# Opening of a two-layer expert and attention kernel: layer statistics of tiles 2 to 4 set earlier on VectorE, one weight row of the first tile spread by ScalarE, and ScalarE's copy of w2 set behind it

## What is computed

```python
def expert_layer(xt):                       # xt: 8192 x 128, normalised
    scores = sigmoid(xt @ gate_w.T)         # 16 experts
    _, idx = top_k(scores + gate_b, 4)
    w = take_along_axis(scores, idx)
    w = w / sum(w) * 2.5
    comb = zeros(T, 16).at[rows, idx].add(w)
    y = 0
    for e in range(16):
        gate, up = split(xt @ w13[e].T)     # 64 each
        y = y + comb[:, e] * ((silu(gate) * up) @ w2[e].T)
    return y + shared_expert(xt)

x = x + 0.5 * expert_layer(layernorm(x))
x = x + attention(layernorm(x))
x = x + 0.5 * expert_layer(layernorm(x))
```

## Time and profile before

| | |
|---|---|
| median of 3 runs | 842.72 us (842.61 to 843.36) |
| the profiled execution | 843.58 us, of which its span is 841.8 us |
| TensorE busy | 828.7 us (98%) |
| VectorE busy | 723.9 us (86%) |
| ScalarE busy | 528.0 us (63%) |
| GpSimd busy | 613.4 us (73%) |
| TensorE's granted clock | full in all 40 slices of the span |

### The profile page before, as it was taken

How to read it: one execution, slowest core, us unless ns; L and a number is a source line. 1 busy time by engine, 2 the same in 40 slices (tenths; PEclk the granted TensorE clock), 3 DMA queues, 4 the chain that set the end, 5 groups by cost and what they waited for, 6 DMA issues and landing times.

```text
span 841.8 us, 16377 instructions
## 1 busy us (share of the span) xinstructions
PE 828.7 (98%) x4345; PEld 689.8 (82%) x4345; DVE 723.9 (86%) x2118; ACT 528.0 (63%) x1049; POOL 613.4 (73%) x560
## 2 busy tenths in 40 slices
PE   8899999999999999999999999999999999999998
PEld 7777888888888877888999999788888888888886
DVE  6989999989998988778887776899998999998886
ACT  5555666656666577676776766666656656666564
POOL 6767777777677678888888883567777777777664
PEclk9999999999999999999999999999999999999999
DMA  5787766666676634433333430566666555555553
GB/s 187 208 245 197 196 177 164 178 164 180 181 180 175 164 96 108 127 108 102 95 97 104 126 101 1 131 165 161 156 159 158 148 155 140 139 154 143 148 146 82
DMA packets 69377, 123.09 MB, mean 146 GB/s; under 512 B 8784, under 2 KB 19904, under 8 KB 69056
## 3 DMA queue, kind: packets, MB, share of 16 engines
q1 hardware_dynamic: 69312, 122.33, 54.1%
HBM read 104.28 MB, written 9.63 MB: 135 GB/s over the span
## 4 chain that ended last, share of the span: by engine, by line
PE 88%; DVE 2%; DMA 2%; ACT 1%; issue 1%; SPq 0%; DVEq 0%; ACTq 0%; POOL 0%; POOLq 0%
PE bank L1551 82%; PE bank L1877 3%; PE bank L1668 1%; DMA comb_rows<-combT 1%; PE bank L1660 1%; DMA qkT<-comb_rows 1%; ACT probT L724 1%; DVE probT L1145 0%; PE bank L1652 0%; SPq L389 0%; DMA stage<-stage 0%; DVE prob L1135 0%; DVE xl L1395 0%; DVE marked L1101 0%; PE bank L1829 0%
## 5 line engine op out<-in xcount | busy, mean ns | idle before, releaser
L511 POOL TENSOR_TENSOR h_l<-probT,h_h 128x512 fp32r<-128x512 f32 x254 | 329.8, 1299 | 175.2 <-ACT h_h L724 175.1
L724 ACT ACTIVATE h_h<-probT 128x512 fp32r<-128x512 f32 (+1 forms) x286 | 179.6, 628 | 79.4 <-DVE probT L1145 76.2
L1551 PE MATMUL bank<-xh,w_h 128*128 128x512 f32 x544 | 220.4, 405 | 2.4 <-DVE prob L1135 1.9
L777 ACT ACTIVATE bank<-bank 128x512 f32<-128x512 f32 x252 | 146.8, 582 | 120.4 <-PE bank L1551 119.9
L1551 PE MATMUL bank<-xh,w_l 128*128 128x512 f32 x544 | 214.8, 395 | 0.0
L1551 PE MATMUL bank<-xl,w_h 128*128 128x512 f32 x544 | 214.5, 394 | 0.0
L1135 DVE TENSOR_TENSOR prob<-bank,qkT 128x512 f32<-128x512 f32 x252 | 172.9, 686 | 35.7 <-ACT bank L777 29.1
L1145 DVE TENSOR_TENSOR probT<-prob,bank 128x512 f32<-128x512 f32 x255 | 174.0, 682 | 15.8 <-POOL h_l L511 2.9
L1551 PEld LDWEIGHTS bank<-xh,w_h 128*128 128x128 f32 x544 | 102.2, 188 | 27.9 <-DVE prob L1135 3.6
L1551 PEld LDWEIGHTS bank<-xh,w_l 128*128 128x128 f32 x544 | 102.0, 188 | 23.8
L1551 PEld LDWEIGHTS bank<-xl,w_h 128*128 128x128 f32 x544 | 102.4, 188 | 21.1
(11 more groups left out here) (133 smaller groups left out, 1331.1 us busy)
## 6 DMA issues: line engine op xcount, KB each, us to landing
qkT<-comb_rows SPq DMA_DIRECT2D x190, 256.0 KB, 5.3
qkT<-comb_rows SPq DMA_DIRECT2D x124, 128.0 KB, 2.9
rows<-comb_rows SPq DMA_DIRECT2D x28, 512.0 KB, 7.4
stage<-stage SPq DMA_DIRECT2D x64, 128.0 KB, 2.7
X<-in_x SPq DMA_DIRECT2D x16, 256.0 KB, 7.4
stage<-in_x_t SPq DMA_DIRECT2D x16, 256.0 KB, 7.5
x_t<-stage SPq DMA_DIRECT2D x16, 256.0 KB, 2.1
out_x_t<-stage SPq DMA_DIRECT2D x15, 256.0 KB, 2.0
```

The costliest lines, as they stand in the source:

```text
L511: nc.gpsimd.tensor_tensor(lo, f, hi.bitcast(F32), ALU.subtract).then_inc(done, 1)
L724: return nc.scalar.activation(dst, src, ACT.Copy)
L777: nc.scalar.activation(bank[:, G_BANK[g], :], bank[:, G_BANK[g], :], ACT.Silu).then_inc(silu_done, 1)
L1551: return nc.tensor.matmul(dst, lhsT, rhs, start=start, stop=stop)
```

## The change

It has four parts, all of them in the opening. (1) GpSimd's first root is made in two halves with semaphores of its own (first_root, first_var, first_rstd), VectorE normalises tile 0 in two halves (first_xn) and TensorE's transposes start at the first. (2) The statistics of tile 1 stand ahead of that on VectorE, those of tile 2 ahead of xl(0), and those of tile 3 (T = 3, the fourth tile) behind xl(0) instead of in tile 0's row of work; the four loads of x move up in the list of loads, and ScalarE makes xh(0) ahead of its copy of the second part of w13. (3) ON_DVE is 1: spread row 1 is now made by ScalarE from comb, behind the normalisation of tile 1. (4) ScalarE's copy of w2 moves from behind the normalisation of tile 1 to behind xh(1). The counts of waits that the removed neg_mean and neg_shift of tile 0 had fed are lowered by one (pool_count).

```diff
-ON_DVE = 2
+ON_DVE = 1
...
             load(X[:, 0:NB, :], x_v[:, 0:NB, :], x_loaded[0])
+            load(X[:, NB:2 * NB, :], x_v[:, NB:2 * NB, :], x_loaded[1])
             load(ident[:], ident_d, gate_loaded)
             load(gw_f[:], gwT, gate_loaded)
             load(gb[:], gate_b, gate_loaded)
             load(w13_f[:, early[0], :], w13T[:, early[0], :], w13_loaded[0])
-            load(X[:, NB:2 * NB, :], x_v[:, NB:2 * NB, :], x_loaded[1])
+            load(X[:, 2 * NB:3 * NB, :], x_v[:, 2 * NB:3 * NB, :], x_loaded[2])
             load(w13_f[:, early[1], :], w13T[:, early[1], :], w13_loaded[1])
-            load(X[:, 2 * NB:3 * NB, :], x_v[:, 2 * NB:3 * NB, :], x_loaded[2])
+            load(X[:, 3 * NB:4 * NB, :], x_v[:, 3 * NB:4 * NB, :], x_loaded[3])
             load(w13_f[:, early[2], :], w13T[:, early[2], :], w13_loaded[2])
             load(w2_f, w2T, w2_loaded)
-            load(X[:, 3 * NB:4 * NB, :], x_v[:, 3 * NB:4 * NB, :], x_loaded[3])
...
+            def first_root():
+
+                pool.wait_ge(mv_done, 1)
+                nc.gpsimd.tensor_tensor(var_eps[:, 0:NB], mv[:, 0:NB, 1], eps[:, 0:NB], ALU.add).then_inc(first_var, 1)
+                pool.wait_ge(first_var, 1)
+                for a in range(2):
+                    at = slice(NB // 2 * a, NB // 2 * (a + 1))
+                    nc.gpsimd.tensor_tensor(rstd[:, at], var_eps[:, at], neg_half[:, at], ALU.pow).then_inc(first_rstd, 1)
...
-                    ffn_rstd(base)
-                    pool.wait_ge(xn_done, 1)
+                    first_root()
+                    pool.wait_ge(first_xn, 2)
...
                     copy(w13_h[:, early[0], :], w13_f[:, early[0], :]).then_inc(w13_hi[0], 1)
+                    opening_xh(base, 0)
                     act.wait_ge(w13_loaded[1], 16)
                     copy(w13_h[:, early[1], :], w13_f[:, early[1], :]).then_inc(w13_hi[1], 1)
-                    opening_xh(base, 0)
...
                     for n in range(NB):
                         ffn_xn(base + 1, 1, n)
-                    act.wait_ge(w2_loaded, 16)
-                    copy(w2_h[:], w2_f).then_inc(w2_hi, 1)
+                    comb_spread(1)
                     ffn_combT(base, 0)
                     comb_spread(2)
                     opening_xh(1, 1)
+                    act.wait_ge(w2_loaded, 16)
+                    copy(w2_h[:], w2_f).then_inc(w2_hi, 1)
                     ffn_silu(base, 0, 3)
...
                     ffn_xl(N, 1 - q)
-                    dve.wait_ge(x_loaded[3], 16)
-                    ffn_stats(L, Lx, 1 - q)
                     ffn_weighted(T, q, 2)
...
-                dve.wait_ge(rstd_done, 1)
-                ln_apply(NB, 0, xn_done)
-                dve.wait_ge(x_loaded[1], 16)
-                ffn_stats(1, 1, 1)
-                ffn_stats_wait(1)
-                ffn_mv(1, 1)
                 ffn_xl(0, 0)
-                dve.wait_ge(x_loaded[2], 16)
-                ffn_stats(2, 2, 0)
+                dve.wait_ge(x_loaded[3], 16)
+                dve.wait_ge(mv_done, 2)
+                ffn_stats(3, 3, 1)
...
                 comb_spread(0)
-                comb_spread(1)
                 ffn_comb(0)
...
                 else:
                     pe.wait_ge(spread_copied, j - ON_DVE + 1)
-                    pe.wait_ge(weighted_done, 1 if j == 2 else j)
+                    wait(pe, weighted_done, (0, 0, 1, 3)[j])
```

More of the change, by code:

```diff
@@ L236, in macaron @@
         neg_shift_done = sem("neg_shift_done")
+        first_var = sem("first_var")
+        first_rstd = sem("first_rstd")
         rows_loaded = sem("rows_loaded")
@@ L241, in macaron @@
         xT_copied = sem("xT_copied")
+        first_xn = sem("first_xn")
         xn_done = sem("xn_done")
@@ L326, in ln_count, with pool_count @@
             return T - (1 if base else -1)
+        def pool_count(T, base):
+            return ln_count(T, base) - 1
         def opening_count(T):
@@ L728, in ffn_xn @@
                 if n == 0:
-                    act.wait_ge(neg_shift_done, opening_count(T))
+                    act.wait_ge(neg_shift_done, opening_count(T) - 1)
                     act.wait_ge(xnT_ready, opening_count(T) - 1)
@@ L1204, in ffn_tile @@
                     ffn_xl(N, 1 - q)
-                    dve.wait_ge(x_loaded[3], 16)
-                    ffn_stats(L, Lx, 1 - q)
                     ffn_weighted(T, q, 2)
                     ffn_stats_wait(L)
-                    dve.wait_ge(var_done, 2)
-                    dve.wait_ge(neg_mean_done, 2)
+                    dve.wait_ge(var_done, 1)
+                    dve.wait_ge(neg_mean_done, 1)
                     ffn_mv(L, 1 - q)
@@ L1313, in ffn_start @@
                 ffn_mv(0, 0)
+                dve.wait_ge(x_loaded[1], 16)
+                ffn_stats(1, 1, 1)
+                for a in range(2):
+                    dve.wait_ge(first_rstd, a + 1)
+                    ln_apply(NB // 2, NB // 2 * a, first_xn, NB // 2 * a)
+                ffn_stats_wait(1)
+                ffn_mv(1, 1)
+                dve.wait_ge(x_loaded[2], 16)
+                dve.wait_ge(mv_done, 1)
+                ffn_stats(2, 2, 0)
                 dve.wait_ge(gw_hi, 1)
                 low_half(gw_hl[:, NEXP:2 * NEXP], gw_f[:], gw_hl[:, 0:NEXP], gw_split)
-                dve.wait_ge(rstd_done, 1)
-                ln_apply(NB, 0, xn_done)
-                dve.wait_ge(x_loaded[1], 16)
-                ffn_stats(1, 1, 1)
-                ffn_stats_wait(1)
-                ffn_mv(1, 1)
                 ffn_xl(0, 0)
-                dve.wait_ge(x_loaded[2], 16)
-                ffn_stats(2, 2, 0)
+                dve.wait_ge(x_loaded[3], 16)
+                dve.wait_ge(mv_done, 2)
+                ffn_stats(3, 3, 1)
                 ffn_stats_wait(2)
-                dve.wait_ge(xn_done, 1)
-                dve.wait_ge(var_done, 1)
-                dve.wait_ge(neg_mean_done, 1)
+                dve.wait_ge(first_xn, 2)
+                dve.wait_ge(first_var, 1)
                 ffn_mv(2, 0)
@@ L1631, in ffn_xnT @@
             def ffn_xnT(T):
-                pe.wait_ge(xn_done, opening_count(T))
+                if T:
+                    pe.wait_ge(xn_done, opening_count(T) - 1)
                 wait(pe, combT_done, T)
                 for n in range(NB):
+                    if T == 0 and n % 2 == 0:
+                        pe.wait_ge(first_xn, n // 2 + 1)
                     ins = nc.tensor.transpose(bank[:, T_BANK, n * P:(n + 1) * P], xn[:, n, :], ident[:])
@@ L1649, in ffn_combT @@
                 if ahead:
-                    pe.wait_ge(rstd_done, ln_count(T + 2, base))
-                    pe.wait_ge(neg_mean_done, ln_count(T + 2, base))
+                    pe.wait_ge(rstd_done, pool_count(T + 2, base))
+                    pe.wait_ge(neg_mean_done, pool_count(T + 2, base))
                 nc.tensor.transpose(bank[:, T_BANK, 0:P], comb[:].rearrange("p e n -> p (e n)"),
```

8 lines of the change are left out of this document (4 added, 4 removed).

## The result

| | before | changed |
|---|---|---|
| median of 22 runs each | 843.43 us (842.01 to 846.40) | 845.43 us (844.24 to 847.02) |
| the profiled execution | 843.58 us, span 841.8 | 845.75 us, span 843.9 |

The ratio is 1.0018 (95%: 1.0010 to 1.0026): the change makes the kernel 2.0 us slower. The prediction was 844.6 us, +1.9 on the median it started from. Over more runs the kernel before came out at 843.43, not 842.72, so the sum is compared by its difference. Single runs lie up to 3.0 us from their median in the kernel before and up to 1.6 us in the changed one.

The account below looks back on a forecast made before the run. It took TensorE to bound the kernel, gapless from 30 us on, so only the opening counted. +2.32 - 0.32 - 0.10 = +1.9 us took the median from 842.72 to 844.6 us; eight-in-ten range 843.5 to 845.5.

Parts of the forecast that it names:

- the sum: Lateness of TensorE at G(6) of tile 0: +2.32 - 0.32 - 0.10 = +1.9 us, everything else costed at nothing.
- The front: Opening up to xh(1): xl(0) 0.69 us earlier, at about 8.5; 0.30 of it left at xh(1), 18.55.
- the fourth part of x: Load in the opening: lands at about 8.8, up to 9.7 us; routing of tile 0 then starts at 10.5.
- The copy of w2: On ScalarE behind xh(1): starts 2.32 us later, at 19.05, delaying low half of w2, h_l(0), h(2), weighted(4), G(6).
- Rival (b): h buffer of pair 0 free in time, copy doesn't decide; G(6) 0.3 to 0.6 us earlier: 842.1 to 842.4; 8%.
- (d): Ahead of G(6): the change gains over 1.7 us, the whole idle time there; 2%.
- rival (c): TensorE idle before down(0) and G(6): its clock falls to the low level, +3 to +4, 846 to 847 us; 6%.
- a clock under 1.00 from 24 to 34 us: Sign on TensorE around G(6): a granted clock below 1.00 in that window would make the prediction wrong.
- rival (a): Tile 2's wait for spread weights swallows 0.2 us at most: +1.7, 844.4 us; counted in the forecast, no chance of its own.
- the border between slower and same: Whole time: 0.2% of 842.72, 1.7 us, so slower lies above 844.4; slower 0.65, same 0.33.

Follow-up runs that it names:

- w2_mid: Changed kernel with ScalarE's copy of w2 directly behind spread row 1, ahead of combT(0): 843.07 us, ratio 0.9996 to the kernel before.
- tab_after: Changed kernel with the two 1 MB rotation table loads moved to tiles 10 and 11: 844.91 us, ratio 1.0011 to the kernel before.
- w2_only: Kernel before with one edit, ScalarE's copy of w2 moved behind xh(1): 845.46 us, ratio 1.0030 to the kernel before.
- fill10: Changed kernel with 10 idle 128x128 matmuls in TensorE's wait before G(6): 845.25 us, ratio 1.0024 to the kernel before.
- tab_fill10: Changed kernel with rotation tables loaded at tiles 10 and 11 and 10 idle matmuls before G(6): 844.27 us, ratio 0.9999 to the kernel before.
- w2_back: Changed kernel with the copy of w2 back behind xn of tile 1, ahead of spread row 1: 844.88 us, ratio 1.0013 to the kernel before.
- tab_after2: Changed kernel with rotation tables loaded at tiles 10 and 11, measured beside changed_again: 844.78 us, ratio 1.0009 to the kernel before.
- changed_again: The changed kernel itself, unedited, measured again on chip 10: 846.19 us, ratio 1.0028 to the kernel before.
- fill: Changed kernel with 20 idle 128x128 matmuls in TensorE's wait before G(6): 847.51 us, ratio 1.0045 to the kernel before.
- front_only: Kernel before with parts 1 and 2 of the change alone, spread row 1 and the w2 copy where they were: 842.83 us, ratio 0.9993.

## Why the prediction was right, and where it was not

**The front.** xl(0) was put at about 8.5 and stands at 8.51; xh(1) at 18.55 and 18.60. Only 0.25 us of the front's 0.68 reaches xh(1), as spread row 1 takes ScalarE's time. In six of the ten other profiles with this front VectorE waited 0.40 to 1.07 us for the fourth part of x. In w2_mid it could start on it only at 10.21, in tab_after at 10.48, so its landing, put at 8.8 to 9.7, can cost more than was allowed.

**The copy of w2.** Predicted 19.05, low half 20.3, h(2) 24.2, weighted(4) 28.3, G(6) 29.05; measured 19.09, 20.33, 24.25, 28.35 and 29.09. That this chain, and not another part, makes the loss is shown: alone it gives +2.1 (w2_only), and with the copy moved up again the loss is gone (w2_mid). Rival (b), that the copy doesn't decide, is out, and so is (d).

**What was mis-sized.** The sum ended at G(6) and took TensorE to be without a gap from 30 us on. Two terms behind it were wrong, and in the profiled pair they cancel almost: 0.8 lost, 1.1 returned. First, rival (c): the clock fell. The prediction had named a clock under 1.00 from 24 to 34 us as a sign of being wrong, and it was 0.83. It gave this 6%, while all but one of the 22 runs of the changed kernel show a clock under 0.999; and it priced it at +3 to +4 in all, while TensorE lost 0.8 in the profiled execution, and the whole time shows nothing of it (fill10) to 0.5 (tab_fill10). The Trainium skill, "TensorE: Matmul & The Clock Gate", section "HAM oscillation", ties the low clock to idle gaps beyond a certain length. The runs agree in kind, as 2.4 us of waiting was mostly followed by a fall, but the length of the one gap doesn't decide it here: 1.70 us in w2_back and 1.25 in w2_only were followed by a fall as well, and the 2.40 us of tab_after2 was not.

Second, rival (a): tile 2 can take in "that 0.2 at most". The step that failed is the reading of TensorE's windows: the ones shown ended at 60 and began again at 66 us, and the stretch left out held most of the stall. The tile's period of 21.49 us against 19.33 would have given 2.16 us. Against it the changed kernel came 1.1 us nearer in the profiled pair and 1.9 in changed_again. But the stall varies from one execution to the next: 0.2 to 2.2 us above 19.33 in the nine profiles with early tables, and in fill and front_only the tile behind was long too (20.80 and 20.12). w2_mid and front_only reach combT(2) as early as the kernel before and have 0.5 and 0.2. So it is not shown that the stall is shorter because TensorE comes later, and the 1.1 us may be mostly the long tile 2 of one execution of the kernel before. That the clock's fall and the stall are both there, and that the stall goes with the tables, is shown; how far they balance is not settled to better than half a us.

**The total.** +2.0 measured, +1.9 predicted. The chain was right in mechanism and size; that the rest came to nothing was partly luck. The median itself, 845.43, lies at the upper edge of the stated 843.5 to 845.5, since the base stood 0.7 higher than its first three runs had it. The prediction took 0.2% as the border between slower and same and gave slower 0.65; the ratio of 1.0018 lies just under that border, and its interval on both sides.

## What to carry to other kernels

When a copy is moved on an engine, follow what stands behind its consumer: here ScalarE's w2 copy held GpSimd's low half, that held the first h_l behind it in GpSimd's list, and that a buffer VectorE needed; the slack was 0.32 us and the move 2.3. A tile's period, taken from one mark per tile, shows a stall that windows with modelled matmul ends hide, and a stall behind the change may return part of the loss, which one pair of profiles can't size. Large loads that nobody needs yet should not be issued just ahead of a small write that somebody waits for: moving them took the stall away in all five profiles, and 0.5 to 1.4 us off the medians, not each beyond the noise.

## What the runs showed of the hardware

- TensorE's clock fell after an idle 2.4 us in most executions (after, changed_again and tab_after, but not tab_after2), and in other kernels after 1.70 us (w2_back) and 1.25 us (w2_only). What it costs depends on the place: nothing where TensorE waited again behind it (w2_only), nothing to half a us in the whole time at G(6), and 1.6 us at logits(1) in w2_back, where VectorE waited for the slowed matmuls.
- A write of 36 KB took 4.1 to 5.9 us with two 1 MB loads issued some 8 us ahead of it (nine profiles), and 1.8 to 2.5 us without them (five).
- A root by power of 2 columns took about 0.70 us (two in 1.39 in the changed kernel), 0.72 by the estimate from the rows of 4 and 8 columns.
- A 128x128 float matmul used as filler took 0.22 us (twenty in 4.39, fill).
